# A two-layer MetaFormer kernel on one core: the front redrawn in six units, tap stores paced by the expert pairs, and the loops over expert chunks 1 to 4 written out

## The chip, the cores and the metric

One core of one Trainium2 chip runs the whole kernel in one launch. The metric is the device time of an execution in microseconds (us). Before the change three runs gave 1070.49, 1071.0 and 1072.88 us, median 1071.0.

## The reference, cut to what matters

The input is `x`, f32, 8 x 64 channels x 64 x 64. Two layers are computed, each with a mixer and a routed expert block, both added to `x`:

```python
x = x + _L0_conv_ref(_ln_c(x), L0_conv_kernel_base)      # spectral convolution
t = t + _L0_ffn_ref(_ln_t(t), ...)                       # 8 experts, top 2
x = x + _L1_conv_ref(_ln_c(x), L1_conv_kernels)          # depthwise, up to 29 x 29
t = t + _L1_ffn_ref(_ln_t(t), ...)
```

`_ln_c` and `_ln_t` subtract the mean over the 64 channels and divide by the standard deviation. The spectral convolution takes a 2D Fourier transform, keeps the frequencies up to 16, multiplies each kept frequency pair by a 64 x 64 complex matrix `kernel_base[r2]`, where `r2` is the sum of the two squared frequencies, and transforms back. The expert block sends each of 32768 tokens through the best two of eight 64 x 64 matrices and adds the two results with their gate weights.

## The kernel before, in words

Everything is written by hand for four compute engines (PE, DVE, ACT, POOL) and the DMA queue of SP; each engine runs its own list, and semaphores tie them together. Nothing is scheduled by a planner: the order in the code is the order on the engine.

**The front.** `x` comes in twice, once as `x_rows` (into `X`, for the statistics of the layer norm) and once as `x_chan` (into `R1`, as weights for PE), each 8 MB, in four pieces of 2 MB, only the first `x_rows` piece in two halves. SP issues all loads at once, in the order rows 0, constants, rows 1, channels 0, rows 2, channels 1, rows 3, channels 2, channels 3. The transform over one axis is cut into 32 groups n (8 per piece). For each, four f32 matmuls fill a PSUM bank (L1330, `c_dft`); DVE multiplies by the reciprocal root (L734, `scale_columns`); POOL adds the mean to the constant column (L488, `centre_columns`); ACT writes the f16 high part (L1053); POOL, or DVE for odd n from 17 on, writes the low part (L448, L741). Four banks are used: PE may be four groups ahead of L734. The statistics are 256 `bn_stats` on DVE (L720), 64 per piece, and of each piece POOL and ACT make root and mean in ten short steps (`piece_root`, L462 to L479, with `piece_seed`, L1070 to L1075), placed after groups 3, 7 and 15. `piece_root` stands on POOL in one block, so that groups wait behind it.

From n = 24 on, each group of the first transform is followed on PE by one of the 16 groups of the second (L1345), whose f16 high and low parts ACT (L1061) and DVE (L749) make; its banks are 4 to 7. Two memsets on POOL (L506, L509) clear the room of the mixing matrices, ACT and DVE turn them into f16 halves (`row_high`, L1097; `row_low`, L766; `last_high_part`, L1087; `last_low_part`, L758). The mixing matrices come by `spec_re` and `spec_im` in many small transfers. After the last group of the second transform PE mixes: 1014 small matmuls (L1367), which the whole rest of the kernel waits for.

**Expert blocks.** Tokens are worked in 8 chunks per layer, of 16 pairs each. A pair: PE computes seven expert differences (L1480, L1481), DVE weighs them out of PSUM (L891, counted in `y_used`), POOL adds the products twice (L565, L575), PE sums with the token (L1492, L1495). Between pairs DVE also computes the gates of the next chunk and the statistics of the chunk after that (L707). Chunk 0 and chunks 5 to 7 are written out, chunks 1 to 4 are a loop of two rounds, two chunks per round, on each of PE, DVE, ACT and POOL:

```python
expert_chunk(layer, 0, 0, True, True, True)
with dve.Fori(0, 2) as m:                 # L1038; POOL L630, ACT L1297, PE L1574
    expert_chunk(layer, 2 * m + 1, 1, True, True, True)
    expert_chunk(layer, 2 * m + 2, 0, True, True, True)
expert_chunk(layer, 5, 1, True, True, False)
```

**Tap stores.** In chunk 0 of layer 0 DVE turns the taps of the second convolution into f16 halves (L925, L928, L931). SP then stores 128 shifted windows of them to DRAM (L406, 458.5 KB each), as fast as the queue takes them. They are loaded back (L414) only after layer 0's last chunk.

Of the kernel before, what the change touches and what calls it, by code (L numbers as in the profile page):

```python
# [16 lines left out]
P = 128  # L17
# [50 lines left out]
def metaformer(nc, x_chan, x_rows, x_tok, spec_re, spec_im, dft, dft16, inv_h, inv_c, ident, ident16,  # L68
               experts0, experts1, rank, taps, out):
    ctx = ExitStack()  # L70
    with ctx:
# [94 lines left out]
        first_in = sem("first_in")  # L166
        xb_in = [sem(f"xb_in{i}") for i in range(4)]
        xr_in = [sem(f"xr_in{i}") for i in range(4)]
# [72 lines left out]
        NPIECE = 4  # L241
# [34 lines left out]
        ROOT_AFTER = {3: 1, 7: 2, 15: 3}  # L276
# [18 lines left out]
        def matrix_runs(t):  # L295

            runs = []
            for slot, (a, b) in enumerate(matrices(t)):
                if runs and runs[-1][1] == a:
                    runs[-1][3] += 1  # L300
                else:
                    runs.append([slot, a, b, 1])
            return runs

# [3 lines left out]
        def k_in_count(t):  # L308
            return sum(32 * len(matrix_runs(n)) for n in range(t % 3, t + 1, 3))
# [40 lines left out]
        def _(sp):  # L350
# [3 lines left out]
            half_piece = PC // 2  # L354
            sp.dma_start(X[:, 0:half_piece], x_rows[:, 0:half_piece]).then_inc(first_in, 16)
            sp.dma_start(X[:, half_piece:PC], x_rows[:, half_piece:PC]).then_inc(xr_in[0], 16)
            sp.dma_start(dft_sb[:, :], dft).then_inc(dft_in, 16)
            sp.dma_start(rank_sb[:, :], rank).then_inc(rank_in, 16)
            sp.dma_start(X[:, piece(1)], x_rows[:, piece(1)]).then_inc(xr_in[1], 16)
            sp.dma_start(xb[:, piece(0)], x_chan[:, piece(0)]).then_inc(xb_in[0], 16)  # L360
            sp.dma_start(X[:, piece(2)], x_rows[:, piece(2)]).then_inc(xr_in[2], 16)
            sp.dma_start(xb[:, piece(1)], x_chan[:, piece(1)]).then_inc(xb_in[1], 16)
            sp.dma_start(X[:, piece(3)], x_rows[:, piece(3)]).then_inc(xr_in[3], 16)
            sp.dma_start(xb[:, piece(2)], x_chan[:, piece(2)]).then_inc(xb_in[2], 16)
            sp.dma_start(dft16_sb[:, :], dft16).then_inc(const_in, 16)
            sp.dma_start(xb[:, piece(3)], x_chan[:, piece(3)]).then_inc(xb_in[3], 16)
# [4 lines left out]
            lo, hi = BLOCKS  # L371

            sp.dma_start(last_raw[lo, 0:17, 0:64], spec_re[:, 16, :, :]).then_inc(last_in, 16)
# [8 lines left out]
            for t in range(NSTEP):  # L382
                if t == 0:
                    sp.wait_ge(c_dft, 24)
                if t >= 3:
                    sp.wait_ge(k_low, 2 * (t - 2))
# [1251 lines left out]
```

## Time and profile before

| | us |
|---|---|
| median of 3 runs | 1071.0 |
| the profiled execution's own time | 1070.98 |
| its span (first to last instruction) | 1069.2 |
| front, to the first mixing matmul | 99.4 |
| mixing | 99.4 to 130.9 |
| rest of the spectral convolution, to the first expert pair | 130.9 to 234.8 |
| expert chunks of layer 0 | 234.8 to 508.3 |
| depthwise convolution on PE | 537.6 to 764 |
| expert chunks of layer 1 | 805.3 to 1056.3 |

The program spends 1.8 us outside of the span. The boundaries are starts of instructions in the trace; the chunks' are the starts of L891. PE is busy for 84% of the span, DVE for 75%, but which of them a stage waits for differs from stage to stage, and has to be read there.

### The profile page before, as it was taken

The numbers are of one execution on the slowest core, as the hardware profiler recorded it, in microseconds if no ns is written. First come the engines' busy times: TensorE is split into PE (matmuls) and PEld (weight loads), VectorE is DVE, ScalarE is ACT, GpSimd is POOL, SyncE is SP. The second block draws the span as 40 slices with busy tenths as digits, with TensorE's granted clock in tenths as the row PEclk, the third lists the DMA queues.
The fourth block names the chain that finished last, engine by engine and source line by source line (L and its number), as shares of the span: only waits on it lengthen the run. The fifth ranks groups of instructions, "written<-read, shape, count | busy, mean of one in ns | idle before, by whom it ended". The sixth has DMA issues, their size and how long they took to land.

```text
span 1069.2 us, 26695 instructions
## 1 busy us (share of the span) xinstructions
PE 895.9 (84%) x9610; PEld 725.5 (68%) x9610; DVE 801.9 (75%) x1954; ACT 512.1 (48%) x1074; POOL 596.7 (56%) x564
## 2 busy tenths in 40 slices
PE   2994999758997899988289999999537999999987
PEld 2994988745664566655189999999524666666655
DVE  7746676879896787999766667675557988887783
ACT  1447554585665466510044444444167666566400
POOL 1861000518886688777374333440065888888876
PEclk9998599977999899999689999999857999999999
DMA  9866200021999995000468878778000100001100
GB/s 389 303 213 229 66 2 1 2 47 71 391 395 398 397 397 208 2 1 1 161 225 269 269 264 275 262 266 271 9 1 1 41 35 27 39 20 41 41 40 40
DMA packets 49973, 163.30 MB, mean 153 GB/s; under 512 B 9952, under 2 KB 12128, under 8 KB 48096
## 3 DMA queue, kind: packets, MB, share of 16 engines
q1 hardware_dynamic: 49888, 162.21, 42.0%
q8 instruction: 48, 0.79, 0.3%
q14 instruction: 37, 0.30, 0.1%
HBM read 93.70 MB, written 68.49 MB: 152 GB/s over the span
## 4 chain that ended last, share of the span: by engine, by line
PE 39%; POOL 28%; issue 15%; DVE 10%; ACT 4%; DMA 2%; POOLq 1%; SPq 0%; DVEq 0%; ACTq 0%
PE pair L1540 21%; POOL R L565 14%; POOL R L575 8%; PE pair L1444 4%; PE pair L1495 3%; PE pair L1367 3%; DVE R L891 2%; PE pair L1492 2%; DMA X<-x_rows 2%; DVE work L707 2%; POOL R L448 2%; PE pair L1480 1%; ACT pair L1180 1%; PE pair L1481 1%; PE pair L1555 1%
## 5 line engine op out<-in xcount | busy, mean ns | idle before, releaser
L891 DVE TENSOR_TENSOR R<-pair,R 128x896 f32<-128x896 f32 x256 | 276.0, 1082 | 68.7 <-PE pair L1481 59.5
L565 POOL TENSOR_TENSOR R<-R 128x768 f32<-128x768 f32 x128 | 234.3, 1831 | 100.3 <-DVE R L891 98.8
L1540 PE MATMUL pair<-R 128*128 (+4 forms) x2880 | 226.8, 243 | 19.7 <-DVE R L945 19.7
L1540 PEld LDWEIGHTS pair<-R 128*128 128x128 f16 x2880 | 224.2, 98 | 22.2 <-issue 19.8
L1180 ACT ACTIVATE pair<-X,work 128x64 f32 (+1 forms) x496 | 171.8, 395 | 128.9 <-DVE R L831 123.8
L1480 PE MATMUL pair<-work,R 128*128 128x448 f16 x512 | 186.0, 363 | 53.5 <-DVE R L891 51.2
L1481 PE MATMUL pair<-work,R 128*128 128x448 f16 x512 | 185.0, 361 | 0.0
L575 POOL TENSOR_TENSOR R<-R 128x512 f32<-128x512 f32 x128 | 163.3, 1276 | 12.7 <-POOL R L565 5.2
L954 DVE COPY R<-R 128x1152 f32<-128x1152 f32 x64 | 92.3, 1444 | 76.8 <-PE pair L1540 76.0
L1245 ACT COPY R<-R 128x1152 f32<-128x1152 f32 x64 | 82.1, 1284 | 125.1 <-PE pair L1540 125.1
L1495 PE MATMUL pair<-R,ident_sb 128*128 128x256 f32 x512 | 136.0, 389 | 0.0
L1480 PEld LDWEIGHTS pair<-work,R 128*128 128x128 f16 x512 | 50.5, 99 | 121.0 <-DVE R L891 91.4
L1495 PEld LDWEIGHTS pair<-R,ident_sb 128*128 128x128 f32 x512 | 100.6, 196 | 14.7
L595 POOL TENSOR_TENSOR R<-X,R 128x1024 f32<-128x1024 f32 x16 | 46.7, 2920 | 113.1 <-DVE R L945 97.1
L1216 ACT ACTIVATE X<-pair 128x512 f32<-128x512 f32 (+1 forms) x64 | 37.7, 588 | 127.7 <-PE pair L1500 127.7
L1492 PE MATMUL pair<-X,inv_h_sb 128*128 128x256 f32 (+1 forms) x256 | 87.1, 423 | 5.4 <-POOL R L575 5.4
L1458 PE MATMUL pair<-ident_sb,R 128*128 128x128 f16 x512 | 43.0, 232 | 51.0 <-DVE R L831 36.3
L1458 PEld LDWEIGHTS pair<-ident_sb,R 128*128 128x128 f16 x512 | 35.8, 104 | 65.1 <-DVE R L831 54.5
L707 DVE BATCH_NORM_STATS2 work<-X 128x6 f32<-128x64 f32 (+1 forms) x512 | 72.2, 211 | 3.8 <-issue 3.6
L1330 PE MATMUL pair<-dft_sb,R 128*128 128x68 f32 x256 | 56.8, 423 | 19.2 <-DMA R<-x_chan 19.2
L1481 PEld LDWEIGHTS pair<-work,R 128*128 128x128 f16 x512 | 50.9, 99 | 29.4 <-issue 2.2
L1330 PEld LDWEIGHTS pair<-dft_sb,R 128*128 128x128 f32 x256 | 55.5, 332 | 19.3 <-issue 19.2
(132 smaller groups left out, 1397.9 us busy)
## 6 DMA issues: line engine op xcount, KB each, us to landing
taps_halves<-R SPq DMA_DIRECT2D x128, 458.5 KB, 6.5
R<-taps_halves SPq DMA_DIRECT2D x64, 917.0 KB, 4.8
R<-x_chan SPq DMA_DIRECT2D x4, 2048.0 KB, 29.3
X<-x_tok SPq DMA_DIRECT2D x4, 2048.0 KB, 15.3
out<-X SPq DMA_DIRECT2D x16, 512.0 KB, 2.6
X<-x_rows SPq DMA_DIRECT2D x3, 2048.0 KB, 20.0
X<-x_rows SPq DMA_DIRECT2D x2, 1024.0 KB, 6.0
R<-taps SPq DMA_DIRECT2D x2, 603.0 KB, 6.7
```

The costliest lines, as they stand in the source:

```text
L565: pool.tensor_tensor(pr[:, :, 192:384], pr[:, :, 0:192], pr[:, :, 192:384], ALU.add).then_inc(half_ready, 1)
L575: pool.tensor_tensor(w, pr[:, :, 192:320], pr[:, :, 320:448], ALU.add).then_inc(quarter_ready, 1)
L707: last = dve.bn_stats(stat[:, 32 * q + t, :], X[:, bass.ds(k * CT * C + t * C, C)])
L891: dve.tensor_tensor(pr.rearrange("p t (e c) -> p t e c", c=C), pair[p % 2][:, :].rearrange("p (t e c) -> p t e c", t=2, c=C)[:, :, 0:NE - ...
L954: dve.tensor_copy(block_words(j, 0), band_words(i, 0)).then_inc(blocks_ready, 1)
L1180: last = act.activation(xn_psum[:, t * C:(t + 1) * C], X[:, bass.ds(k * CT * C + at * C, C)], ACT.Identity, bias=small[2 * q][:, at:at + 1 ...
L1330: mm = pe.matmul(bank[n % 4][:, j * 68:(j + 1) * 68], xb[:, (4 * n + j) * P:(4 * n + j + 1) * P], dft_sb[:, :], start=True, stop=True)
L1480: pe.matmul(dst, u[q][:, t * P:(t + 1) * P], wa[:, 0:EW], start=True, stop=False)
L1481: mm = pe.matmul(dst, vh[q][:, t * P:(t + 1) * P], wb[:, 0:EW], start=False, stop=True)
L1492: pe.matmul(bank[7][:, 256 * i:256 * (i + 1)], ident_scaled, X[:, bass.ds((k * NOCT + o) * 512 + 256 * i, 256)], start=True, stop=False)
L1495: pe.matmul(bank[7][:, 256 * i:256 * (i + 1)], ident_sb[:, :], w[:, :, j, :], start=False, stop=False)
L1540: mm = pe.matmul(acc[:, y0:y1, x0:x1, :], blocks[i % 2][:, ks, 2 - y, 1 - x, :], src[:, y0 + y:y1 + y, x0 + x:x1 + x, :], start=(ks == 0 a ...
```

## The change

1. **Loads in units.** Pieces 0 and 1 are halved: six units, of 1, 1, 1, 1, 2 and 2 MB (4, 4, 4, 4, 8 and 8 groups). The order is rows 0, constants, channels 0, rows 1, channels 1, rows 2, rows 3, channels 2, rows 4, channels 3, channels 4, rows 5, channels 5.
2. **More banks.** The first transform uses all 8 banks for n < 24, so that PE may be 8 groups ahead of the scaling; the second transform starts at n = 27 in place of 24.
3. **Roots in parts.** The ten steps are divided over four groups on POOL and ACT.
4. **Matrices laid out by the host.** `spec_pairs` holds the 136 matrices in the order in which they are used, 2 transfers per step; the last row and column (`spec_last`) come ahead of the constants.
5. **Tap stores paced.** Store p waits until `y_used` is at least 4 + 7p//8.
6. **Loops written out.** `for m in range(2)` in place of `Fori(0, 2)`, in both layers, on all four engines.

```diff
-        ROOT_AFTER = {3: 1, 7: 2, 15: 3}
+        UNITS = ((0, 0, 32), (0, 32, 64), (1, 0, 32), (1, 32, 64), (2, 0, 64), (3, 0, 64))
+        UNIT_AT = {0: 0, 4: 1, 8: 2, 12: 3, 16: 4, 24: 5}
+        ROOT_FROM = {0: 1, 4: 2, 8: 3, 12: 4, 20: 5}
+        FIRST_H = 27
...
+        def c_dft_bank(n):
+            return bank[n % 8 if n < 24 else n % 4]
...
             for p in range(P):
                 at = (WI - 1 - p // HI) * PITCH + HI - 1 - p % HI
+                sp.wait_ge(y_used, 4 + 7 * p // 8)
                 sp.dma_start(taps_dram[:, :, p, :].rearrange("s c n -> (s c) n"),
...
-                        sp.dma_start(k_raw[t % 3][r, slot:slot + n], spec_re[:, a, b:b + n, :]).then_inc(k_in[t % 3], 16)
+                    sp.dma_start(k_raw[t % 3][r], spec_pairs[:, PER_STEP * t:PER_STEP * t + PER_STEP, :]
+                                 ).then_inc(k_in[t % 3], 16)
...
             for n in range(32):
                 scale_columns(n)
-                if n < 16:
-                    piece_stats(2 + n // 8, 8 * (n % 8), 8 * (n % 8) + 8)
...
+                if n < 8:
+                    unit_stats(2 + n // 4, 8 * (n % 4), 8 * (n % 4) + 8)
+                elif n < 12:
+                    unit_stats(4, 16 * (n - 8), 16 * (n - 8) + 16)
+                elif n < 20:
+                    unit_stats(5, 8 * (n - 12), 8 * (n - 12) + 8)
+                if n >= FIRST_H + 2:
+                    h_dft_low_part(n - FIRST_H - 2)
...
-                if n >= 4:
-                    pe.wait_ge(c_dft_scaled, n - 3)
+                if n >= 8:
+                    pe.wait_ge(c_dft_scaled, n - 7 if n < 28 else n - 3)
...
-                with dve.Fori(0, 2) as m:
+                for m in range(2):
                     expert_chunk(layer, 2 * m + 1, 1, True, True, True)
                     expert_chunk(layer, 2 * m + 2, 0, True, True, True)
```

**PE at the start of the front**, before; L1330 and L1349 are the first transform, and `c_dft_scaled` counts the groups that DVE has scaled:

```order
L1330 MATMUL pair<-dft_sb,R 128x68 [waits xb_in0,dft_in]
L1330 MATMUL pair<-dft_sb,R 128x68 x15
L1330 MATMUL pair<-dft_sb,R 128x68 [waits c_dft_scaled]
L1330 MATMUL pair<-dft_sb,R 128x68 x3
L1330 MATMUL pair<-dft_sb,R 128x68 [waits c_dft_scaled]
```

and now:

```order
L1349 MATMUL pair<-dft_sb,R 128x68 [waits xb_in0,dft_in]
L1349 MATMUL pair<-dft_sb,R 128x68 x15
L1349 MATMUL pair<-dft_sb,R 128x68 [waits xb_in1]
L1349 MATMUL pair<-dft_sb,R 128x68 x15
L1349 MATMUL pair<-dft_sb,R 128x68 [waits c_dft_scaled,xb_in2]
```

PE has 8 groups of four matmuls before it waits for DVE, where it had 4.

**DVE behind the last statistics**, before. L734/L740 scale, L741/L747 and L749/L755 are low parts of the first and the second transform, L758/L764 is the low half of the last matrices:

```order
L720 BN_STATS work<-X 128x6 x8
L734 TENSOR_TENSOR R<-pair,work 128x272 [waits c_dft_low,c_dft,piece_step]
L734 TENSOR_TENSOR R<-pair,work 128x272 [waits c_dft_low,c_dft] x2
L741 TENSOR_TENSOR R<-R 128x68x4 [waits c_dft_high]
L734 TENSOR_TENSOR R<-pair,work 128x272 [waits c_dft_low,c_dft] x2
```

and now:

```order
L726 BN_STATS work<-X 128x6 x8
L747 TENSOR_TENSOR R<-R 128x68x4 [waits c_dft_high]
L740 TENSOR_TENSOR R<-pair,work 128x272 [waits c_dft_low,c_dft]
L740 TENSOR_TENSOR R<-pair,work 128x272 [waits c_dft_low_v,c_dft_low,c_dft]
L747 TENSOR_TENSOR R<-R 128x68x4 [waits c_dft_high]
L740 TENSOR_TENSOR R<-pair,work 128x272 [waits c_dft_low_v,c_dft_low,c_dft] x2
L747 TENSOR_TENSOR R<-R 128x68x4 [waits c_dft_high]
L740 TENSOR_TENSOR R<-pair,work 128x272 [waits c_dft_low,c_dft_low_v,c_dft,piece_step]
```

The last statistics stand before the scaling of n = 16 in the old order, and before n = 20 in the new one; the wait for the last root (`piece_step`) stands at n = 24 in both.

**DVE where chunk 1 of layer 0 begins**, before:

```order
L891 TENSOR_TENSOR R<-pair,R 128x896 [waits y_ready]
L1038 UNCONDITIONAL_BRANCH
L1038 ISA
L887 ISA [waits gate_step]
L889 ISA [waits y_ready]
L891 TENSOR_TENSOR R<-pair,R 128x896 [waits quarter_ready]
L705 ISA
L707 ISA [waits tok_step]
L707 BN_STATS work<-X 128x6
L707 ISA
L707 BN_STATS work<-X 128x6
```

and now:

```order
L904 TENSOR_TENSOR R<-pair,R 128x896 [waits y_ready]
L904 TENSOR_TENSOR R<-pair,R 128x896 [waits quarter_ready,y_ready,gate_step]
L714 BN_STATS work<-X 128x6 [waits tok_step]
L714 BN_STATS work<-X 128x6 x3
L904 TENSOR_TENSOR R<-pair,R 128x896 [waits y_ready]
```

The branches are gone, and so are the instructions that only compute the loop's addresses and counts.

## Rows read from the trace of the kernel before

**Rows 1.** The page's first line.
```profile
span 1069.2 us, 26695 instructions
```
**Rows 2.** Stretches A:B: length, busy PE, PEld, DVE, ACT, POOL, clock, DMA share, GB/s.
```profile
5.70:19.18 13.48, 0.00 (x0) 0.03 (x1) 13.48 (x107) 1.10 (x4) 3.15 (x10) 1.00 1.02 427
57.50:80.40 22.90, 22.90 (x180) 22.64 (x179) 11.76 (x21) 10.96 (x18) 15.14 (x19) 1.00 0.73 253
99.38:130.90 31.52, 30.74 (x1014) 30.19 (x1014) 21.19 (x26) 19.25 (x25) 0.00 (x0) 0.50 0.34 91
```
**Rows 3.** Instructions of PE in time (start us, duration us), front.
```profile
19.18 5.15 PE L1330 MATMUL pair<-dft_sb,R 128*128 128x68 f32 x23 [19.18 <-DMA R<-x_chan]
...
89.31 5.20 PE L1345 MATMUL pair<-dft_sb,R 128*128 128x68 f16 x87 [8.89 <-DVE R L741]
...
99.38 0.79 PE L1367 MATMUL pair<-R 128*128 128x16 f16 x21 [3.45 <-DVE R L749]
```
**Rows 4.** Groups of the front: line, engine, names, xcount | busy us, mean ns | idle.
```profile
L1330 PE MATMUL pair<-dft_sb,R 128*128 128x68 f32 x256 | 56.8, 423 | 19.2 <-DMA R<-x_chan 19.2
...
L720 DVE BATCH_NORM_STATS2 work<-X 128x6 f32<-128x64 f32 x256 | 33.9, 209 | 7.3 <-DMA X<-x_rows 7.3
L448 POOL TENSOR_TENSOR R<-R 128x272 f16<-128x272 f32 x24 | 23.3, 970 | 0.8 <-ACT R L1053 0.8
...
L734 DVE TENSOR_TENSOR R<-pair,work 128x272 f32<-128x272 f32 x32 | 13.5, 429 | 8.4 <-POOL R L448 5.1 <-issue 2.8 <-PE pair L1330 0.4
...
L506 POOL MEMSET R<- 128x4352 f32 x1 | 3.7, 3724 | 0.0
```
**Rows 5.** First and last of the ten steps of piece 3's root on POOL.
```profile
50.88 0.38 POOL L462 TENSOR_TENSOR work<-work 128x64 f32<-128x64 f32 x1
...
55.37 0.32 POOL L479 TENSOR_TENSOR work<-work 128x64 f32<-128x64 f32 x1
```
**Rows 6.** DVE scales groups 23 and 24.
```profile
65.46 0.78 DVE L734 TENSOR_TENSOR R<-pair,work 128x272 f32<-128x272 f32 x2
```
**Rows 7.** Stretches: chunks 1, 2, 3, 5 of layer 0 and 3 of layer 1.
```profile
274.80:306.80 32.00, 29.45 (x275) 20.09 (x273) 28.39 (x67) 20.32 (x55) 26.65 (x27) 1.00 1.03 395
306.80:342.90 36.10, 31.45 (x311) 21.50 (x307) 28.43 (x67) 23.80 (x63) 29.85 (x29) 1.00 1.03 396
342.90:380.60 37.70, 30.47 (x239) 20.10 (x240) 28.52 (x67) 16.95 (x46) 23.77 (x25) 0.86 1.03 397
...
413.00:444.30 31.30, 29.45 (x281) 20.31 (x278) 24.64 (x36) 19.64 (x52) 24.92 (x18) 1.00 0.09 32
...
904.50:936.50 32.00, 29.46 (x279) 20.25 (x277) 28.42 (x67) 20.26 (x55) 26.73 (x27) 1.00 0.08 33
```
**Rows 8.** DVE at the end of the loop's first round, layer 0 and then layer 1.
```profile
342.90 1.09 DVE L891 TENSOR_TENSOR R<-pair,R 128x896 f32<-128x896 f32 x1 [4.16 <-POOL R L575]
343.91 0.34 DVE L707 BATCH_NORM_STATS2 work<-X 128x6 f32 x2
347.89 0.35 DVE L707 BATCH_NORM_STATS2 work<-X 128x6 f32 x2 [3.64 <-issue]
...
904.53 1.09 DVE L891 TENSOR_TENSOR R<-pair,R 128x896 f32<-128x896 f32 x1 [0.66 <-PE pair L1481]
905.54 0.59 DVE L707 BATCH_NORM_STATS2 work<-X 128x6 f32 x4
```
**Rows 9.** DMA queues between 274 and 413 us (packets, MB, share of 16 engines).
```profile
q14 instruction: 12, 0.10, 0.2%
```
**Rows 10.** The tap stores: issue ns, first and last issue, time to landing.
```profile
L406 SPq DMA_DIRECT2D taps_halves<-R x128: 353/1114/2958, 261.7 to 411.3; - x128
...
DMA to landing us min/median/max: 2.5/6.5/15.6
```
**Rows 11.** First and last of 16 eight-column matmuls of PE in a row.
```profile
338.99 0.17 PE L1468 MATMUL pair<-work,R 128*128 128x8 f16 x1
...
339.37 0.17 PE L1469 MATMUL pair<-work,R 128*128 128x8 f16 x1
```

More of the change, by code:

```diff
@@ L165, in metaformer @@
         rank_in = sem("rank_in")
-        first_in = sem("first_in")
-        xb_in = [sem(f"xb_in{i}") for i in range(4)]
-        xr_in = [sem(f"xr_in{i}") for i in range(4)]
+        xb_in = [sem(f"xb_in{i}") for i in range(6)]
+        xr_in = [sem(f"xr_in{i}") for i in range(6)]
         x_in = sem("x_in")
@@ L308, in k_in_count @@
         def k_in_count(t):
-            return sum(32 * len(matrix_runs(n)) for n in range(t % 3, t + 1, 3))
+            return 32 * (t // 3 + 1)
+        def c_dft_bank(n):
+            return bank[n % 8 if n < 24 else n % 4]
         def mixed_count(item):
@@ L448, in c_dft_low_part, with unit_root @@
                 pool.tensor_tensor(out_, src, high_, ALU.subtract).then_inc(c_dft_low, 1)
-            def piece_root(i):
+            def unit_root(i, part):
                 base = i * PIECE_STEPS
-                stats = piece_stat[i % 2]
-                shift, root = small[i % 2], small[2 + i % 2]
-                total, gap, spread, t, seed = small[4:9]
+                piece, g0, g1 = UNITS[i]
+                at = slice(g0, g1)
+                stats = piece_stat[piece % 2][:, at, :]
+                shift, root = small[piece % 2][:, at], small[2 + piece % 2][:, at]
+                total, gap, spread, t, seed = (m[:, 0:g1 - g0] for m in small[4:9])
@@ L759, in last_low_part, with row_low @@
                                          op0=ALU.mult, op1=ALU.subtract).then_inc(last_low, 1)
-            def row_low(t):
+            def row_low(t, parts=(0, 1)):
                 raw, row = k_raw[t % 3], k_row[t % 3]
-                for i, r in enumerate(BLOCKS):
+                for i in parts:
+                    r = BLOCKS[i]
                     dve.wait_ge(k_high, 2 * t + i + 1)
@@ L1037, in _ @@
                 expert_chunk(layer, 0, 0, True, True, True)
-                with dve.Fori(0, 2) as m:
+                for m in range(2):
                     expert_chunk(layer, 2 * m + 1, 1, True, True, True)
@@ L1296, in _ @@
                 expert_chunk(layer, 0, 0, True, True, True)
-                with act.Fori(0, 2) as m:
+                for m in range(2):
                     expert_chunk(layer, 2 * m + 1, 1, True, True, True)
@@ L1573, in _ @@
                 expert_chunk(layer, 0, 0, True, True)
-                with pe.Fori(0, 2) as m:
+                for m in range(2):
                     expert_chunk(layer, 2 * m + 1, 1, True, True)
@@ L1614, in host_layout @@
     taps[:, (CENTRE - d[None, :] * PITCH - d[:, None]).reshape(-1)] = np.asarray(kernels).reshape(C, -1)
-    return dict(x_chan=c(xc), x_rows=c(xr), x_tok=c(xt), spec_re=c(mats[0]), spec_im=c(mats[1]), dft=dft,
+    return dict(x_chan=c(xc), x_rows=c(xr), x_tok=c(xt), spec_pairs=c(pairs), spec_last=c(last), dft=dft,
                 dft16=dft16, inv_h=inv_h, inv_c=inv_c, ident=eye, ident16=eye.astype(np.float16),
```

265 lines of the change are left out of this document (135 added, 130 removed).

## The prediction

> **What bounds the kernel now.** I read the busy time in stretches first. There is no single bound: PE, DVE and POOL take turns. So each part of the change has to be priced in its own stage, and a microsecond won at a place through which everything passes is won to the end. There are two such places. The first mixing matmul at 99.38 us [rows 3] is one: it needs the whole front, and all that follows hangs on it. The expert chunks are the other: they follow each other without slack.
>
> In the front, PE does nothing until 19.18 us, and the row names the load of `x_chan` as what it waits for [rows 3], while the queue is full, at 427 GB/s [rows 2]. Once PE has begun it is busy without a gap to 80.4 [rows 2], then waits 8.89 us for the low part of the last group, then 3.45 us more for the last DVE part before the mixing [rows 3]. So the front is late at its head (the order of the loads) and at its tail (the round through DVE, POOL, ACT and DVE).
>
> In the expert chunks, one chunk of the loop takes 32.0 us in layer 0 (chunk 1) and the same in layer 1 (chunk 3), although stores run at 395 GB/s beside the first and hardly a transfer beside the other [rows 7]. The stores as such cost the chunk nothing. But chunk 2 of layer 0 takes 36.1 and chunk 3 takes 37.7 us with the same busy time of DVE (28.4 and 28.5) [rows 7]. The excess, 4.1 + 5.7 = 9.8 us, lies around the jump back to the loop's head: DVE stands still for 4.16 us before its first multiplication, starts two statistics, and stands still 3.64 us more, for nothing that the profile shows ("issue") [rows 8]. The same jump in layer 1 shows 0.66 us, ended by PE, and no such hole [rows 8]. Between the two only the traffic differs. I read the holes as instructions that have to be fetched anew behind a full DMA queue.
>
> **The front, worked out.** Head: 1 MB (1.05 million bytes) at 427 GB/s takes 2.5 us. The first MB of rows is there at 5.7 us, where DVE's stretch begins [rows 2]; now the first MB of channels is next, so PE starts at about 8.5 in place of 19.18. It needs 56.8 / 32 = 1.78 us per group [rows 4]; a piece more arrives every 5 us (1 MB of rows, 1 MB of channels) and feeds four groups, 7.1 us, so PE doesn't wait for loads again. With eight banks it runs through n = 27, the 28th group, by about 58.
>
> Middle: now DVE is late. From 5.7 it has 33.9 us of statistics, 20 of the 32 scalings (20 / 32 x 13.5 = 8.4) [rows 4] and some 4 us of holes (the second MB, the first roots), so the last statistics end at 52. Then comes the root of the last unit. In one block it took 50.88 to 55.69, 4.8 us [rows 5]. In parts, between the memset of 3.7 us, of which some 2 are left at 52, and two low parts of 23.3 / 24 = 0.97 [rows 4], it is done at about 60. Group 24 is scaled at 60.3, against 66.2 now [rows 6]: **5.9 us gained**.
>
> Tail: from there the old order took 99.38 - 66.2 = 33.2 us. In it PE had 7 first-transform groups (12.4 us), 15 or 16 second-transform groups (0.74 each where they run densely, 5.20 / 7 [rows 3]; 11.5), and 12.3 us of the two waits above. Now PE has only 4 groups of the first (28 to 31, 7.1) and 15 of the second (11.1), 18.2 us. I add waits: the second transform's groups 5 to 8 need low parts that DVE makes behind the last matrices' 2.5 us, some 3.3 us in sum, 2 of small joints, and 1.4 between the last group and the mixing, since `row_low` is split and no longer stands right before the last parts. That is 24.9 us in place of 33.2, **8.3 us gained**. The mixing starts at 85.2, 14.2 earlier. I walked all four lists with these durations; the same walk of the old lists gives a start within 1 us of the trace's, and that is my error bar on this term, doubled for what is new in the order.
>
> The memsets and roots stay on POOL, and they are covered as long as PE has its banks; without them each microsecond of POOL there would show. The mixing itself is not shortened: PE is busy for 30.7 of 31.5 us [rows 2]. Its matrices now come by 2 transfers a step. That costs and gives nothing, since PE waits for none of them. `x_tok` (8 MB, 20 us at this rate) is issued at about 52 and is there at 77, over 80 us before its first reader. The six units add four transfers on SP's queue, behind which nothing waits that isn't there in time.
>
> **The stores.** Pacing moves the last of them from 411.3 [rows 10] to pair 115 of 128, about 24 us before the layer's last pair; with at most 15.6 us to landing [rows 10] they are done before the loads that need them. Cost 0; what stands behind them on SP waits for the end of the layer anyway. What they do is thin the traffic, from 395 to about 8 x 0.47 MB per 14 us, 270 GB/s.
>
> **The loops.** Written out, there is no jump back and so nothing to fetch anew. Chunks 2 and 3 of layer 0 fall to 32.2 each: 73.8 - 64.4 = **9.4 us gained**. In layer 1 the rows show nothing to gain: the chunks inside the loop cost 32.0, there is no hole at the jump [rows 7, 8], and the address instructions that vanish were covered. Bound from below: some other engine's share of these, 0; from above, 0.7 us per chunk, the difference of a chunk of the loop to chunk 5, which is straight code [rows 7]; that would be 5.6 us in eight. I take 0, since chunk 5 has no statistics to make (24.6 us of DVE against 28.4 [rows 7]), which explains the difference.
>
> Here the Trainium skill speaks ("Runtime: NRT & Kernel Launch", section on instruction fetch mechanics): prefetch is sequential, and a taken branch to a page that isn't held forces a fetch before execution goes on. By that rule alone layer 1 stalls too; the trace disagrees for the quiet queue (0.66 us at the jump [rows 8]).
>
> **The sum.** Against the profiled execution, 1070.98 us (span 1069.2 [rows 1]), two hundredths from the median of 1071.0: 1070.98 - 5.9 - 8.3 - 9.4 = 1047.4 us. A measurement of this kernel tells about 0.2% (2 us) from no change.
>
> **Rivals.**
>
> (a) *The tail stays long.* If DVE and ACT, with 16 high parts and 16 low parts to make, set the pace of the second transform as before, the 8.3 us don't come: 1055.7. For it: in the old tail PE waited for them. Against: PE waited at a place (the change from the first half to the second, 8.89 us) where the last group's chain was queued behind eight parts and a matrix; now five stand there.
>
> (b) *The holes stay.* If what stalls is not the jump but any fetch behind stores, chunks 2 and 3 stay at 73.8: 1056.8. Against: chunk 1, also full of stores, is straight code in its first round and takes 32.0 [rows 7].
>
> (c) *The clock.* The mixing runs at a granted clock of 0.50 [rows 2], 1.2 GHz, at 31.5 / 1014 = 31.1 ns per matmul; to 80.4 it is 1.00 [rows 2], and then come the idle stretches. At full clock small matmuls follow each other by (339.37 - 338.99) / 15 = 25.3 ns [rows 11]. If PE, no longer idle for 9 us there, kept 2.4 GHz, the mixing would be 1014 x 5.8 ns = 5.9 us shorter: 1041.5. Against: it stayed low through 31 us in which PE was hardly idle, so the mixing itself doesn't seem to raise it.
>
> (d) *Jumps cost in both layers*, hidden in layer 1 in places that I don't see: another 9.4 us, 1038.0. This is what the skill's rule would give. Little speaks for it.
>
> (e) *Slower.* The written-out code has to be fetched once more for each chunk, and the paced stores now run beside all eight chunks of layer 0, not beside four. Twelve fetches of this queue fell in the 139 us with stores [rows 9]; over the 8 chunks it would be about 24. If each held an engine on the path for the 3.64 us of [rows 8], they would cost 87 us; from 7 such stalls on, 25.5 us, more than the 23.6 gained, the kernel is slower, and with 8 it is at 1076.5. Against it stands chunk 1 again, with its fetches under full load and no hole.
>
> **How the numbers follow.** Forecast 0.65, with its own range of 1043.5 to 1051; (a) 0.12; (b) 0.07; (c) 0.07; (d) 0.05; (e) 0.04. The likeliest time is 1047.4. The range reaches from (c) to (b), 1041.5 to 1057, and leaves out (d) and (e) and the edges of the others. Faster by over 0.2%: all cases but (e), and a hundredth for gains that are given back: 0.95. Same 0.01, slower 0.04.
>
> **What would show it.** PE's first matmul at 8 to 9 us; group 24 scaled near 60; the first mixing matmul at 84 to 87; the mixing still 31 to 32 us at clock 0.50; eight chunks of layer 0 with no hole of DVE over 1 us that ends in "issue", chunks 1 to 4 at 32 to 32.5; chunks of layer 1 unchanged; the last store 20 us or more before the layer's end. A first transform that pauses for loads, a root of the last unit later than 63, or chunks of layer 0 over 33 us would make it wrong.

## The result, and the profile after

The changed kernel takes 1045.32 us (median of 4 runs, 1044.47 to 1046.51) against 1071.66 for the kernel before beside it (4 runs, 1070.49 to 1072.88): a ratio of 0.9756, 95% interval 0.9741 to 0.9772. It is faster by 26 us. The forecast was 1047.4, from a range of 1041.5 to 1057.

The profiled execution took 1045.68 us. Stretches in the two traces; group 24 is taken at the end of its scaling, and a layer's chunks run from the start of the first expert pair to the end of the last:

| | before | after | gained to here |
|---|---|---|---|
| first matmul of PE | 19.18 | 9.13 | 10.1 |
| group 24 scaled | 66.2 | 59.7 | 6.5 |
| first mixing matmul | 99.38 | 84.72 | 14.7 |
| first expert pair, layer 0 | 234.77 | 222.60 | 12.2 |
| layer 0, chunks 0 to 7 | 273.5 | 261.7 | 24.0 |
| layer 1, chunks 0 to 7 | 251.0 | 249.5 | 25.5 |

The page's span line, and its rows of the DMA issues:

```profile
span 1043.9 us, 25287 instructions
...
taps_halves<-R SPq DMA_DIRECT2D x128, 458.5 KB, 3.3
...
R<-spec_pairs SPq DMA_DIRECT2D x16, 272.0 KB, 5.1
```

Paced, a tap store lands 3.3 us after its issue. The busy times by stretch, as in [rows 2]: the load, the first transform, the tail, the mixing, the transposes:

```profile
5.70:16.03 10.33, 6.90 (x33) 6.93 (x33) 8.64 (x65) 0.99 (x4) 2.44 (x10) 1.00 1.01 420
9.13:69.27 60.14, 58.46 (x307) 57.90 (x307) 46.09 (x266) 28.19 (x57) 48.40 (x115) 1.00 0.95 343
69.27:84.72 15.45, 8.61 (x153) 7.74 (x154) 13.91 (x26) 13.00 (x25) 2.28 (x5) 1.00 0.99 380
84.72:117.46 32.74, 30.70 (x1014) 30.13 (x1014) 21.40 (x26) 19.89 (x26) 0.00 (x0) 0.54 0.33 88
119.23:130.90 11.67, 10.96 (x136) 10.30 (x136) 8.77 (x8) 8.44 (x9) 0.00 (x0) 0.76 0.01 1
```

PE is busy for 58.5 of 60.1 us of the first transform, so it hardly pauses for loads. In the tail, DVE is now the busiest engine (13.9 of 15.5 us), where before the last groups waited for a round through four engines. The mixing is as much work as before (30.7 us of PE, [rows 2]), but takes 32.7 us. PE's timeline from the end of the second transform on:

```profile
77.36 5.10 PE L1366 MATMUL pair<-dft_sb,R 128*128 128x68 f16 x102 [1.39 <-DVE R L755]
84.72 4.43 PE L1388 MATMUL pair<-R 128*128 128x16 f16 x143 [2.26 <-DVE R L755]
89.40 3.93 PE L1388 MATMUL pair<-R 128*128 128x16 f16 x128 [0.26 <-issue]
93.69 3.99 PE L1388 MATMUL pair<-R 128*128 128x16 f16 x128 [0.36 <-issue]
97.98 4.00 PE L1388 MATMUL pair<-R 128*128 128x16 f16 x128 [0.31 <-issue]
103.09 2.11 PE L1388 MATMUL pair<-R 128*128 128x16 f16 x64 [1.11 <-issue]
```

At first PE stops every 128 matmuls for 0.3 us, and once for 1.11 us, for nothing that the profile shows. Before, the same view had one such joint of 0.55 us, and then 870 matmuls in one row:

```profile
99.38 4.42 PE L1367 MATMUL pair<-R 128*128 128x16 f16 x144 [3.45 <-DVE R L749]
104.36 26.50 PE L1367 MATMUL pair<-R 128*128 128x16 f16 x870 [0.55 <-issue]
```

The root of the last unit on POOL [rows 5] is done in parts, with groups between them:

```profile
55.59 0.20 POOL L498 TENSOR_TENSOR R<-R,work 128x8 f32<-128x8 f32 x1
55.99 0.32 POOL L474 TENSOR_TENSOR work<-work 128x64 f32<-128x64 f32 x1 [0.20 <-ACT work L1084]
56.27 0.88 POOL L452 TENSOR_TENSOR R<-R 128x272 f16<-128x272 f32 x1
57.10 0.48 POOL L498 TENSOR_TENSOR R<-R,work 128x8 f32<-128x8 f32 x1
...
58.93 0.32 POOL L487 TENSOR_TENSOR work<-work 128x64 f32<-128x64 f32 x1
59.33 0.32 POOL L489 TENSOR_TENSOR work<-work 128x64 f32<-128x64 f32 x1
```

The loop chunks, which answer to [rows 7]: chunks 1 to 4 of layer 0, then chunk 1 of layer 1:

```profile
262.10:293.80 31.70, 29.41 (x277) 20.12 (x274) 28.37 (x67) 20.34 (x55) 26.83 (x27) 1.00 0.84 329
293.80:325.50 31.70, 29.41 (x277) 20.13 (x274) 28.37 (x67) 20.33 (x55) 26.81 (x27) 1.00 0.72 282
325.50:357.20 31.70, 29.41 (x276) 20.12 (x274) 28.36 (x67) 20.34 (x55) 26.79 (x27) 1.00 0.67 269
357.20:388.90 31.70, 29.40 (x276) 20.13 (x274) 28.37 (x67) 20.33 (x55) 26.80 (x27) 1.00 0.67 268
...
816.10:847.80 31.70, 29.41 (x277) 20.13 (x274) 28.36 (x67) 20.34 (x56) 26.82 (x27) 1.00 0.09 34
```

All take 31.7 to 31.8 us from start to start, in both layers, beside 329 GB/s and beside 34. The busy times are those of before; what went is idle time. At the place of the jump, DVE now shows 0.44 us in place of 4.16 and 3.64 [rows 8]:

```profile
325.59 1.09 DVE L904 TENSOR_TENSOR R<-pair,R 128x896 f32<-128x896 f32 x1 [0.44 <-issue]
```

### The profile page after: what moved, and what is told of

It reads as the page before. It is cut to its first block, busy times and chain, and to the rows that moved or that the text cites. A ratio compares the mean times of both kernels' runs of the same rounds, so it can differ in the third digit from the quotient of the medians.

```text
span 1043.9 us, 25287 instructions
## 1 busy us (share of the span) xinstructions
PE 890.2 (85%) x9610; PEld 722.4 (69%) x9610; DVE 800.9 (77%) x1954; ACT 513.2 (49%) x1082; POOL 600.4 (58%) x584
## 4 chain that ended last, share of the span: by engine, by line
PE 43%; POOL 27%; DVE 12%; issue 9%; ACT 4%; DMA 3%; SPq 1%; POOLq 0%; DVEq 0%; ACTq 0%
PE pair L1561 22%; POOL R L572 14%; POOL R L582 8%; PE pair L1516 4%; PE pair L1465 4%; DVE R L904 4%; DMA X<-x_rows 3%; PE pair L1388 3%; PE pair L1513 2%; PE pair L1501 2%; DVE work L714 2%; PE pair L1502 2%; ACT pair L1199 1%; PE pair L1576 1%; PE pair L1479 1%
## 5 line engine op out<-in xcount | busy, mean ns | idle before, releaser
L904 DVE TENSOR_TENSOR R<-pair,R 128x896 f32<-128x896 f32 x256 | 275.9, 1082 | 59.9 <-PE pair L1502 52.3
L1199 ACT ACTIVATE pair<-X,work 128x64 f32<-128x64 f32 x496 | 171.7, 395 | 118.0 <-DVE R L844 112.9
L1235 ACT ACTIVATE X<-pair 128x512 f32<-128x512 f32 x64 | 37.7, 589 | 125.4 <-PE pair L1521 125.4
L1513 PE MATMUL pair<-X,inv_h_sb 128*128 128x256 f32 x256 | 86.0, 418 | 5.4 <-POOL R L582 5.4
L714 DVE BATCH_NORM_STATS2 work<-X 128x6 f32<-128x64 f32 x512 | 72.0, 210 | 0.2 <-DVE X L1011 0.2
L1349 PE MATMUL pair<-dft_sb,R 128*128 128x68 f32 x256 | 56.1, 422 | 10.8 <-DMA R<-x_chan 9.6
L1349 PEld LDWEIGHTS pair<-dft_sb,R 128*128 128x128 f32 x256 | 55.2, 332 | 11.1 <-issue 9.1
## 6 DMA issues: line engine op xcount, KB each, us to landing
R<-x_chan SPq DMA_DIRECT2D x4, 1024.0 KB, 13.9
X<-x_rows SPq DMA_DIRECT2D x2, 2048.0 KB, 27.3
```

The source lines that it names most:

```text
L714: last = dve.bn_stats(stat[:, 32 * q + t, :], X[:, bass.ds(k * CT * C + t * C, C)])
L904: dve.tensor_tensor(pr.rearrange("p t (e c) -> p t e c", c=C), pair[p % 2][:, :].rearrange("p (t e c) -> p t e c", t=2, c=C)[:, :, 0:NE - ...
L1199: last = act.activation(xn_psum[:, t * C:(t + 1) * C], X[:, bass.ds(k * CT * C + at * C, C)], ACT.Identity, bias=small[2 * q][:, at:at + 1 ...
L1349: mm = pe.matmul(c_dft_bank(n)[:, j * 68:(j + 1) * 68], xb[:, (4 * n + j) * P:(4 * n + j + 1) * P], dft_sb[:, :], start=True, stop=True)
L1513: pe.matmul(bank[7][:, 256 * i:256 * (i + 1)], ident_scaled, X[:, bass.ds((k * NOCT + o) * 512 + 256 * i, 256)], start=True, stop=False)
```

## The experiments

"Front", "pacing" and "loops" are the three parts of the change. Where profiled executions are compared, it is by span: 1069.2 us before, 1043.9 after.

### The loops alone, and DVE's loop alone

The kernel before with all four loops written out in both layers, and nothing else:

```diff
-                with pool.Fori(0, 2) as m:
+                for m in range(2):
...
-                with dve.Fori(0, 2) as m:
+                for m in range(2):
...
-                with act.Fori(0, 2) as m:
+                for m in range(2):
...
-                with pe.Fori(0, 2) as m:
+                for m in range(2):
```

> The kernel before with only the loops over chunks 1 to 4 written out; front and stores as before, so the stores run at full rate. Theory J (the jump back needs a fetch, and a full DMA queue makes it slow): both holes of DVE in chunks 2 and 3 of layer 0 go, 9.4 us, and 0.35 us in each of the 8 loop chunks for the address instructions, 2.8: 1059.5 us. Rival F (any fetch behind stores stalls, pacing is what helps): chunks 2 and 3 stay near 36 and 38, only the 2.8 come: about 1069. Rival R (address instructions are free): 1062.

Measured: 1056.78 us against 1071.51, ratio 0.9871 (0.9853 to 0.9889). Chunks 1 to 4 took 31.8, 31.8, 32.0 and 31.8 us in layer 0, 31.8 each in layer 1. The holes are gone under stores at full rate, and each chunk in which nothing stalled is shorter than it was in the loop, by 0.2 to 0.6 us and by 0.36 in the mean of layer 1.

By span the gain is 15.0 us, but not all of it belongs to the loops. The chunks give 11.2 us in layer 0 and 1.5 in layer 1. Another 1.4 us lie between the layers: that stretch takes 297.0 us before and 295.6 here, and it is 296.9 to 297.0 in four of this document's traces and 295.2 to 295.6 in the other ten, whatever the edit. In the four, clock 0.50 (1.2 GHz) is granted for 27.3 us just behind layer 0, in the ten for 23.9. The kernel before and the changed kernel both have the longer stretch.

Which engine's loop is it? The same with DVE's alone; PE, ACT and POOL keep theirs:

```diff
-                with dve.Fori(0, 2) as m:
+                for m in range(2):
```

> The kernel before with DVE's loop alone written out, in both layers; PE, ACT and POOL keep their loops, and the stores are not paced. Theory that DVE's own jump back is what stands behind the stores: no hole of DVE in chunks 2 and 3, chunks 2 and 3 of layer 0 take 32.1 us instead of 36.1 and 37.7, the time is 1061.5 to 1062.5. Since PE keeps its address instructions, chunks stay at 32.1, not 31.7. Rival that each of the four engines jumps behind the stores: a hole of 3 to 4 us appears on PE or ACT instead, chunks 2 and 3 of 35 us or more, 1067 to 1071.

Measured: 1056.2 us against 1069.33, ratio 0.9884 (0.9866 to 0.9903). Its span is 1054.2 us, the same as with all four loops written out (1054.2); the intervals of the two ratios overlap. Chunks 2 and 3 of layer 0:

```profile
305.00:336.90 31.90, 29.60 (x280) 20.14 (x278) 28.38 (x68) 20.46 (x56) 26.90 (x28) 1.00 1.03 396
336.90:368.60 31.70, 29.41 (x276) 20.13 (x274) 28.36 (x67) 20.29 (x55) 26.70 (x26) 1.00 1.03 399
```

The start of chunk 3, where the kernel before stood still for 4.16 and 3.64 us:

```profile
335.29 1.08 DVE L891 TENSOR_TENSOR R<-pair,R 128x896 f32<-128x896 f32 x1
336.89 1.09 DVE L891 TENSOR_TENSOR R<-pair,R 128x896 f32<-128x896 f32 x1 [0.51 <-issue]
337.89 0.60 DVE L707 BATCH_NORM_STATS2 work<-X 128x6 f32<-128x64 f32 x4
```

The first half of the expectation held: it is DVE's own jump, under stores at 399 GB/s, and no other engine shows a hole. The second half fell for the most part. I had put the last 0.4 us of a chunk down to PE's address instructions; PE has them here, and the chunks are at 31.7 to 31.9 in layer 0 all the same. In layer 1, where nothing stalls, the four chunks take 31.8, 32.1, 31.7 and 31.8 us: in sum 1.0 us less than before, where all four loops written out give 1.4. So most of this part belongs to DVE's loop as well. DVE is busy for 28.4 of 31.7 us, and its wait before the multiplications is shorter. The 64 multiplications of chunks 1 to 4 of layer 1, in the kernel before, with DVE's loop written out, and with all four:

```profile
L891 DVE TENSOR_TENSOR R<-pair,R 128x896 f32<-128x896 f32 x64 | 69.2, 1082 | 13.6 <-PE pair L1481 13.0 <-issue 0.4
```

```profile
L891 DVE TENSOR_TENSOR R<-pair,R 128x896 f32<-128x896 f32 x64 | 69.2, 1082 | 12.9 <-PE pair L1481 10.8 <-issue 2.0
```

```profile
L891 DVE TENSOR_TENSOR R<-pair,R 128x896 f32<-128x896 f32 x64 | 69.2, 1082 | 12.4 <-PE pair L1481 10.7 <-issue 1.8
```

The profile puts the idle time down to PE, but PE waits for DVE's L891 in turn (its banks), so a delay of DVE can come back to it under PE's name. What vanishes can be counted: in the loop DVE's list has 145 instructions in chunk 1, of which 78 only compute, wait or branch; written out it has 77, of which 10. That these 68 are what costs the 0.25 us or so per chunk is the likely reading; no run takes them out by themselves.

The DMA records of the instruction queues tell more of the big holes. There are two such queues: q8 fetches 16384 bytes at a time and is PE's by its timing, q14 fetches 8192 and serves the others; the trace does not say whom. In the kernel before, q14 fetches at 340.61, 345.88 and 351.07 us, around the two holes. With DVE's loop alone written out it fetches nothing between 329.28 and 376.36, although ACT and POOL jump back in that time. And q8 fetches nothing from 319 to 409 us before, nor from 318 to 398 here, although PE jumps back. So of the four jumps DVE's alone is followed by fetches.

### Pacing alone, and the change without it

The kernel before with the wait before each tap store:

```diff
+                sp.wait_ge(y_used, 4 + 7 * p // 8)
                 sp.dma_start(taps_dram[:, :, p, :].rearrange("s c n -> (s c) n"),
```

> The kernel before with only the stores paced; the loops stay. Theory J: with the queue at two thirds the jump's fetches are short, as in layer 1; chunks 2 and 3 fall to 32 to 33 each, 1062 to 1064 us. If the jump alone made the holes, whatever the traffic: no change, 1071.5. Rival F: also 1062, so this run tells the jump alone from the other two, and e1_loops tells J from F.

Measured: 1064.32 us against 1071.51, ratio 0.9927 (0.9909 to 0.9944). Chunks 2 and 3 took 34.1 and 34.5 us, in place of 36.1 and 37.7; of the holes of DVE that end in "issue", one over 0.8 us is left in them:

```profile
343.41 0.35 DVE L708 BATCH_NORM_STATS2 work<-X 128x6 f32 x2 [0.98 <-issue]
```

It is not the only trace of the jump. The multiplication just before it, at 341.08, comes after 2.23 us under PE's name, where 0.4 to 0.5 us stand at the start of a chunk without a jump, and q14 fetches three times here as well (338.93, 341.59 and 344.46 us). The two chunks are 5.2 us longer than written out, half of the 10.3 that they were before: the jump costs less behind thinner traffic, but it is not free. Of the 7.2 us between the medians the chunks of layer 0 give 5.2; the traces of the two kernels differ by the 1.4 us between the layers as well. And the changed kernel with this wait taken out:

```diff
-                sp.wait_ge(y_used, 4 + 7 * p // 8)
```

> The changed kernel without the wait that paces the stores. Theory J: with no jump the full queue does no harm, 1045.3 us, and chunks 1 to 4 of layer 0 at 31.7. Rival F: holes come back wherever a fetch falls, up to 9.4 us: 1050 to 1055.

Measured: 1046.11 us, ratio 0.9765 (0.9743 to 0.9788), the same as the changed kernel within the intervals; chunks 1 to 4 of layer 0 take 31.8 us. Pacing and writing out pay for the same stall. Once there is no jump, pacing is worth nothing here.

### The front alone, and the front with pacing

The changed kernel with the four loops back and the pacing out:

```diff
-                sp.wait_ge(y_used, 4 + 7 * p // 8)
...
-                for m in range(2):
+                with dve.Fori(0, 2) as m:
```

(and so on POOL, ACT and PE).

> The kernel before with only the front redrawn; loops and unpaced stores as before. The parts are taken to add up: the changed kernel's first expert pair is 12.2 us earlier, so 1059.5 us, with chunks 2 and 3 of layer 0 at 36 and 38 again. If the start of layer 0 earlier against the stores changed the holes, it would be off by some us.

Measured: 1058.68 us against 1071.51, ratio 0.9889 (0.9869 to 0.9908). The mixing starts at 84.65 us, the first expert pair at 222.94; chunks 2 and 3 take 36.3 and 37.0, with this hole:

```profile
335.74 0.35 DVE L713 BATCH_NORM_STATS2 work<-X 128x6 f32 x2 [3.57 <-issue]
```

With the pacing kept and only the loops back:

> The changed kernel with the loops kept: front and paced stores alone. If the parts add: 1071 less 12.3 (front alone) less 6.5 (pacing alone), so 1051.5 to 1053.5, with one DVE hole of about 1 us in layer 0 and chunks 2 and 3 of 34 to 34.5 us. Rival that pacing and the earlier front clash (the first chunk begins 12 us earlier against the loads): 1056 or more with chunks 2 and 3 above 35.5 us.

Measured: 1052.91 us against 1069.33, ratio 0.9848 (0.9832 to 0.9863). Chunks 2 and 3 take 34.1 and 34.4; the largest hole of DVE in them that ends in "issue" is 0.84 us, and two of 2.23 and 2.38 us stand there under PE's name. The parts add. By the ratios the front gives 1.1%, the loops 1.2 to 1.3%, the sum 2.4%, which is the whole change.

### Inside the front: banks, order of the loads, the roots

The changed kernel with four banks for the first transform in place of eight:

```diff
-            return bank[n % 8 if n < 24 else n % 4]
+            return bank[n % 4]
...
-                if n >= 8:
-                    pe.wait_ge(c_dft_scaled, n - 7 if n < 28 else n - 3)
+                if n >= 4:
+                    pe.wait_ge(c_dft_scaled, n - 3)
```

> The changed kernel with four PSUM banks for the first transform, as before, in place of eight. Theory D (in the middle of the front DVE is late, not PE, so PE's lead is not used): group 24 is scaled at 59.7 as in the changed kernel, mixing starts at 84.7, no change, 1045.3 us. Rival P (the eight banks are what carries PE over POOL's memset and the roots): PE stands still behind the last root, mixing starts 3 to 4 us later, 1048 to 1049.

Measured: 1044.08 us against 1070.61, ratio 0.9749 (0.9734 to 0.9764), no slower than with eight. PE is later with its 28th group (60.7 us in place of 57.9), and the mixing starts at 84.70 all the same.

The rows before the channels at the head of the load:

```diff
+            load_rows(1)
             load_channels(0)
-            load_rows(1)
+            load_rows(2)
             load_channels(1)
-            load_rows(2)
             load_rows(3)
```

> The changed kernel with each of the first two MB of channels loaded one place later, behind the next MB of rows: PE starts at 11.5 in place of 9.1, DVE gets its second MB of rows at about 9 in place of 11.5. Theory D: PE's later start costs nothing, DVE's earlier statistics win 1 us, mixing starts at 83.7, 1044.3 us. Rival P (PE's early start is what the front gained): 2.4 us later, 1047.7.

Measured: 1044.68 us, ratio 0.9751 (0.9734 to 0.9767). PE starts at 11.86 us in place of 9.13, and the mixing at 84.94 in place of 84.72: of 2.7 us 0.2 arrive. The run changes two things at once, since DVE's second MB of rows comes earlier: its first scaling begins at 13.93 in place of 15.56, but group 24 is scaled no earlier (59.9, 59.7 in the changed kernel). So with this order of the loads 2.7 us of PE's early start are all but slack. That doesn't hold for the 10 us by which the change starts PE: from 9.13 to 69.27 PE stands still for 1.7 us in all, and no run starts it later than 12.2.

The roots in one block again, still at the same groups:

```diff
-                if n - 3 in ROOT_FROM:
-                    unit_root(ROOT_FROM[n - 3], 3)
                 centre_columns(n)
-                for part in range(3):
-                    if n - part in ROOT_FROM:
-                        unit_root(ROOT_FROM[n - part], part)
+                if n in ROOT_FROM:
+                    for part in range(4):
+                        unit_root(ROOT_FROM[n], part)
...
```

and ACT's two parts (`unit_seed`) likewise.

> The changed kernel with the ten steps of each unit's root in one block on POOL and ACT, as before, at the group where they now begin. Theory D: POOL's waits for ACT (some 1.7 us in each of five roots) come onto the path through scaling; group 24 is scaled at about 65 and mixing starts at 90 to 91, so 1051 us: the cutting into parts is then the largest single piece of the front. If parts don't matter: 1045.3.

Measured: 1049.11 us, ratio 0.9785 (0.9768 to 0.9801). The mixing starts at 88.45, 3.7 us later. This is the one of the three that carries weight, though the interval of its ratio still touches that of the changed kernel (0.9741 to 0.9772). POOL's timeline shows why:

```profile
57.47 0.32 POOL L474 TENSOR_TENSOR work<-work 128x64 f32<-128x64 f32 x1 [0.37 <-ACT work L1082]
58.77 0.29 POOL L477 TENSOR_TENSOR work<-work,rank_sb 128x64 f32<-128x64 f32 x1 [0.98 <-ACT work L1088]
...
60.84 0.21 POOL L498 TENSOR_TENSOR R<-R,work 128x8 f32<-128x8 f32 x1
```

POOL waits twice for ACT within the block, 0.37 and 0.98 us, and the root is done at 60.8 in place of 59.6. In parts, the groups' own work fills these waits (the one left before L474 is 0.20 us). The larger share is what queues behind the block: the next group's centring (L498), which begins at 55.59 in parts, begins at 60.84 here, and ACT's high part and DVE's low part hang on it:

```profile
61.78 0.62 DVE L745 TENSOR_TENSOR R<-R 128x272 f16<-128x272 f32 x1 [5.00 <-ACT R L1064]
```

Group 24 is scaled at 62.7, 3.0 us later than in parts.

### The holes in the mixing

Before each of them a DMA record of queue q8 stands: in the changed kernel the four pauses end 1.3 to 1.6 us after such a fetch has landed. In the changed kernel PE's fetch (one per 16 KB, queue q8) starts at 86.86, 90.96, 95.26, 100.59 and 104.19 us: four or so apart, but for the one of 100.59, which comes 5.3 us after the one before, and 1.4 us after its end PE goes on (103.09). From 97 to 101 us the queue carries the matrices and an expert load:

```profile
97.00:101.00 4.00, 3.69 (x125) 3.59 (x122) 3.91 (x6) 3.06 (x4) 0.00 (x0) 0.50 0.83 248
101.00:105.00 4.00, 2.89 (x97) 2.74 (x95) 1.90 (x5) 1.80 (x3) 0.00 (x0) 0.50 0.02 7
```

The queue's load at the fetch is thus a suspect. I took the expert load away from there, to behind the mixing:

```diff
+            sp.wait_ge(stepped, NSTEP - 1)
```

> The changed kernel with the load of layer 0's expert matrices (520 KB) held until seven mixing steps are done; its first reader comes some 20 us later. Theory Q (PE's hole of 1.1 us at 103 in the mixing is an instruction fetch behind this load and the step's matrices): the hole goes, 1044.2 us. Rival: the hole comes from the matrices' large packets alone and stays, 1045.3.

Measured: 1044.1 us against 1070.61, ratio 0.9745 (0.9732 to 0.9759). The hole near 103 us is gone, but one stands near 90, before any expert load:

```profile
84.72 4.38 PE L1389 MATMUL pair<-R 128*128 128x16 f16 x143 [1.86 <-DVE R L756]
90.58 7.80 PE L1389 MATMUL pair<-R 128*128 128x16 f16 x256 [1.48 <-issue]
98.62 18.34 PE L1389 MATMUL pair<-R 128*128 128x16 f16 x615 [0.23 <-issue]
```

The mixing takes 32.2 us in place of 32.7. The median is 1.2 us below the changed kernel's, the ratios' intervals overlap; no gain is shown.

Then the tail. In the changed kernel DVE's `last_low_part` (2.56 us, begun at 63.97 after 2.44 us of waiting for ACT's half) stands at group 26. Here it stands behind the last rows, ACT's half too, and the loads are in the order rows first:

```diff
-                if n == 26:
-                    last_low_part()
...
             row_low(2)
+            last_low_part()
```

> Tail of the front: in the changed kernel DVE runs the low part of the last columns (one step of 2.56 us on 128x2304) at group 26 and ends the channels' low parts at 84.6 us, where PE has waited 2.26 us. Here this step, and its ACT partner of 2.12 us, stand behind the last rows, where nothing of the mixing's first part reads them. If DVE's and ACT's order is what ends the front: the mixing begins near 81.5 to 82.2 us instead of 84.7, and the time is 1042 to 1043. If PE or the adds of POOL end it: the mixing stays at 84.5 or later, 1045.3. If the moved steps become the next wait (the mixing's last columns then wait for them): the mixing is longer than 33 us and 1045 or more.

The same with the late expert load:

> As the run before, and the expert load that lies beside the mixing (520 KB at 97 to 101 us) is issued behind the mixing. Theory that PE's holes in the mixing are code that arrives late behind large transfers: the hole near 103 us (1.1 us in the changed kernel) goes as it did with the late experts alone, the hole near 90 us, which other kernels showed before any expert load, may stay; mixing 81.5 to 82.2 us, 31.5 to 32.3 us long, time 1041 to 1042. Rival that the holes are unrelated to the load: a hole of 1 us or more near 100 us and the time of the run before.

Measured: 1044.58 us (ratio 0.9772, 0.9756 to 0.9788) and 1043.32 (0.9753, 0.9739 to 0.9766), both against 1069.33. The mixing starts at 83.66 and 83.57: 1.1 us earlier, where 2.5 to 3.2 were expected. Group 27 was scaled at 61.6 in place of 66.9, but group 31 only at 70.6 in place of 71.6, because PE is then what is full (the second of the two with its late expert load; then the changed kernel):

```profile
59.00:70.09 11.09, 11.09 (x93) 11.09 (x93) 5.27 (x12) 7.53 (x15) 7.75 (x14) 1.00 1.02 370
```

```profile
59.00:69.28 10.28, 9.48 (x71) 9.29 (x71) 5.89 (x9) 6.73 (x10) 9.24 (x14) 1.00 1.02 360
```

Here PE's late start (12.1 us, rows first) probably counts, which was slack while DVE was behind. The combination with the channels first was not run. And the holes of the mixing are larger than in the changed kernel. With the expert load in place (the profiled execution took 1047.38 us, 2.8 above this kernel's median, so its holes may be larger than usual):

```profile
90.56 7.82 PE L1386 MATMUL pair<-R 128*128 128x16 f16 x256 [2.50 <-issue]
98.59 3.93 PE L1386 MATMUL pair<-R 128*128 128x16 f16 x128 [0.20 <-issue]
104.24 13.93 PE L1386 MATMUL pair<-R 128*128 128x16 f16 x473 [1.73 <-issue]
```

and without it:

```profile
89.46 11.75 PE L1387 MATMUL pair<-R 128*128 128x16 f16 x384 [1.47 <-issue]
102.04 14.14 PE L1387 MATMUL pair<-R 128*128 128x16 f16 x480 [0.83 <-issue]
```

The hole near 102 is smaller but there, although no expert load runs: "late code behind the expert load" is at most a part of it. No version is faster than the changed kernel by more than the intervals allow.

## Why the prediction was right, and where it was not

**The head.** "PE starts at about 8.5": 9.13. "Through the 28th group by about 58": 57.9. Both are right, and both have some slack, as the runs with rows first and with four banks show: 2.7 us later at the start moved the mixing by 0.2, 2.8 us later at the 28th group by nothing. The prediction priced neither by itself. How much of the 10 us at the head the front needs is open. From 9.13 to 69.27 PE stands still for 1.7 us in all, so a start that is much later than in these runs would delay its last group.

**The middle, 5.9.** Group 24 is scaled at 59.7, forecast 60.3: 6.5 us. The step on which it rests, the root in parts done "at about 60", is there at 59.6, and in one block it costs 3.7 us of mixing start, of which 3.0 are there at group 24.

**The tail, 8.3.** From group 24 to the mixing 25.0 us, forecast 24.9. The two terms together are 14.7, forecast 14.2. Of the 25.0 us PE is busy for 18.1, forecast 18.2; its waits are 4.6 us between groups (3.3 + 2 in the forecast) and 2.3 before the mixing (1.4). Rival (a), a tail that stays long, is out. The prediction's list of the old tail doesn't close, though: 12.4 + 11.5 + 12.3 makes 36.2 us, not 33.2. The trace has 20.1 us of PE's work there and 13.1 of waits, so it counted 3.8 us of work too much and left out a wait of 0.77. The gain did not suffer, since it was taken from the measured 33.2.

**The stores, 0.** Right for what the pacing adds, since with the loops out the kernel without it is as fast. Alone it is not 0 but 7 us, of which layer 0's chunks give 5.2 (268.3 in place of 273.5), from the jump's holes.

**The loops in layer 0, 9.4.** Layer 0's chunks gained 11.8, and **the term for the address instructions, 0, is the one that was mis-sized**. The two stalled chunks fell from 73.8 to 63.5, 10.3 us; chunks 1 and 4 by 0.3 and 0.6; chunk 0 by 0.5, which isn't the loops', since it is as short with the loops kept (39.6 us, the front alone). In layer 1, where I took 0, it is 1.5 us. Of the bounds that I kept, 0 and 0.7 us per chunk, the truth lies between, at 0.36 in layer 1. My reason for the 0 was that chunk 5 has no statistics, which explained its shortness; it explained only a part of it. The expectation of the later run named the wrong engine as well: not PE, but for the most part DVE, the busiest in these chunks next to PE.

**The mechanism of the jump.** That the holes are fetches behind DVE's jump, and that full traffic makes them long, is borne out: writing out DVE's loop alone removes holes and fetches under stores at 399 GB/s, and thinner stores halve the loss. But one reading in it was wrong: "Between the two only the traffic differs." In layer 0 q14 fetches three times between 340 and 352 us. In layer 1 of the kernel before it fetches once (904.80, with DVE at work), and with the front new and the loops kept not at all from 874.81 to 960.89 us, with the second round's start at 886.46. Yet a round has the same 292 instructions of DVE in both layers. So layer 1's jump is cheap at least in part because it is hardly followed by a fetch, and that such a fetch would be cheap on a quiet queue is not shown by any run. Why layer 1 needs fewer stays open.

**What was given back.** Of the 14.7 us at the start of the mixing 12.2 reach the first expert pair. I had the mixing at its old length. It is 1.3 us longer (the holes), and the transposes behind it take 1.0 us longer: the granted clock was 0.50 (1.2 GHz) to 135.3 us before and to 124.9 after, so it ends 5.7 us after the start of the transposes, 119.2, where it ended 2.7 us after 132.6. This part I did not foresee. By sum: 14.7 - 2.5 + 11.8 + 1.5 = 25.5 us, against the spans' 25.3. So the forecast hit within 2 us of the profiled execution partly by luck: it had 2.5 us too little loss, and against it 4.4 us too little gain (0.5 in the front, 2.4 in layer 0, 1.5 in layer 1).

**The rivals.** (b), holes at any fetch, is out for DVE (no hole in chunks with stores at 399 GB/s), and true in a small way for PE in the mixing. (c), full clock in the mixing: 0.54 is granted over it; out. (d), jumps cost in both layers: 1.5 us in layer 1 of the 9.4 that it wanted, and no hole at the jump. Here hangs the rule of the Trainium skill ("Runtime: NRT & Kernel Launch", instruction fetch mechanics) that a taken branch out of the held pages forces a fetch before execution goes on. The traces agree that there are fetches behind a jump and that they can stall. The prediction took layer 1 for a disagreement; it is none, since hardly a fetch is seen there, and no run here can show whether that jump's target was held. (e), written-out code that stalls at each chunk: PE has its fetches in the chunks, and all chunks take 31.7 us.

Of the signs that I had named, group 24 near 60, the mixing begun at 84 to 87 and the last store 20 us or more before the layer's end (26) came. Five were missed by a little: PE's first matmul (9.13 for 8 to 9), the mixing (32.7 us at clock 0.54 for 31 to 32 at 0.50), chunks 1 to 4 (31.8 for 32 to 32.5), chunks of layer 1 "unchanged" (0.2 to 0.5 us shorter), and "no hole over 1 us": one of 1.04 us stands before chunk 7, as it did before.

## What to carry to other kernels

A jump back that is followed by fetches of code can cost several microseconds behind full store traffic (10.3 us in two chunks here, 5.2 behind thinner stores), and another jump of the same loop body next to nothing: look for idle time that ends in "issue", or under a wrong name, at the loop's head, and for records of the instruction queues beside it. Write out the loop of that one engine first, since here DVE's alone gave all of the stall and most of the rest. When two edits repair the same stall (pacing and writing out), price them together, not one after the other. And before an early start is counted as a gain, ask who is late next: 2.7 us of PE's early start were all but slack, the block of root steps that groups queue behind was not.

## What was not expected of the hardware

- **When a fetch has landed, the engine goes on 1.3 to 2.0 us later.** 8 KB packets on q14 landed at 340.94 and 346.24 us before, and DVE resumed at 342.90 and 347.89 [rows 8]; with pacing one landed at 341.95, and DVE resumed at 343.41; with the front alone 334.10, resumed at 335.74. For PE, 16 KB on q8: 101.66, resumed at 103.09 after; 89.08 and 90.58 with late experts; 100.75 and 102.04 in the last run. The packets of these fetches take 0.3 to 0.4 us for 8 KB and 1.1 to 1.3 for 16 KB. So the larger part of a stall is not the transfer: of the 4.16 us, 1.9 pass before the packet starts and 2.0 after it has landed.
- **Straight code of PE can run out as well.** In the mixing 128 matmuls of 31 ns go with each fetch of 16 KB (8 fetches in 33 us), and PE pauses after many of these stretches for 0.2 to 0.4 us, and up to 2.50 us (in a trace of a kernel with the last matrices late) while matrices come in at some 100 to 250 GB/s. "Runtime: NRT & Kernel Launch" of the Trainium skill (instruction fetch mechanics) calls the crossing of such a boundary mostly hidden; that agrees with the expert chunks and not with the mixing. The mixing was 30.7 to 31.5 us long in the kernels that began it near 99 us, and 32.2 to 34.9 in those that began it at 84 to 88. Why the earlier start makes it worse stays open: late experts took away one of the holes, not all.
- **The loops of PE, ACT and POOL cost next to nothing here.** With DVE's loop written out, writing out theirs too leaves the span at 1054.2 us; at most 0.5 us in layer 1's chunks is theirs.
